# The middle tap of a three-tap convolution, moved from VectorE to ScalarE

## The chip, the cores and the metric

The kernel runs on one core of one Trainium2 chip. The metric is the device time of one execution in microseconds (us). Three runs of the kernel before took 1846.09 to 1850.96 us, median 1847.55. A core has five engines that matter here: TensorE (PE: matmuls and transposes), VectorE (DVE), ScalarE (ACT), GpSimd (POOL) and SyncE (SP, which issues DMAs). They run in parallel, each through its own list of instructions in order, and meet at semaphores. Matmul results land in eight PSUM banks; the rest is in SBUF, on 128 partitions.

## What is computed

The input `x` is 8 images of 512 channels and 32x32 tokens, f32. Four residual blocks follow each other, each on a group-normalized `x`: L0 (a 1x1 convolution with 25 correlations added to its inputs), L1 (the block that the change is in), and two plain 1x1 convolutions L2 and L3. L1, cut to what matters:

```python
xz = silu(einsum('oc,bchw->bohw', in_proj_w, x) + in_proj_b)      # 512 -> 1536 channels
x_ssm, res, gate = split(xz, 3, axis=1)
xf = x_ssm.reshape(B, 512, 1024)
xf = conv_general_dilated(xf, dw_w, (1,), [(1, 1)], feature_group_count=512) + dw_b   # 3 taps per channel
xf = silu(xf)
dbc = einsum('oc,bcn->bon', dbc_w, xf) + dbc_b                    # dt, B, C of a selective scan
y = selective_scan(gather(xf), softplus(dt), A, B, C, D)          # over a permutation of the tokens
y = scatter_back(y) * silu(gate) + res
out = silu(einsum('oc,bchw->bohw', out_proj_w, y) + out_proj_b)
```

The convolution of channel c at token n is w0 * x[n-1] + w1 * x[n] + w2 * x[n+1] + b, with zeros outside the 1024 tokens. The middle tap is w1 * x[n] + b.

## The kernel before

Channels lie on partitions, in 4 chunks of 128 (`KC`); tokens lie along the free dimension, 1024 of them, worked on in two halves of 512. The program of each engine is written out by hand, one `image` function per engine, run for images 0 to 7; the middle six run as a loop of two. `wait(eng, name, m, n)` holds an engine until semaphore `name` stands at the n-th event of image m. Nothing schedules: what stands first in an engine's text runs first.

The stage around the change is the head of an image. TensorE multiplies the 1536 output channels of the in projection in 24 units of 128 channels by 512 tokens; a unit is 12 f16 matmuls (`filler(1)`, in `in_step`, line 1467). Units 0 to 7 are `x_ssm`, two for each channel chunk. Between them stand `tokens(0)` to `tokens(3)`: for chunk k, 16 recorded small matmuls with `w_dbc` into bank 0 and 8 transposes (line 1620). Each waits for `conv_act`, the silu of its chunk.

ScalarE evicts each unit from PSUM (`in_evac`, line 599: silu with bias and a scale, into `conv_in`, which lies in `buf_b`, for units 0 to 7; into `gate` and `res` later). Between evictions come `conv_silu(m, k)` (line 607, in place on `conv_out[:, k % 2]`, which lies in `res`) and `tok_evac` (line 612, which copies the transposed tokens to `rows`). After unit 8 come an Exp and a Ln with their table loads (lines 641 and 643), half of the softplus of dt.

VectorE makes the three taps of chunk k, each a pass over 128x1024 f32: middle (line 1144, `tensor_scalar` with w1 and b), left (1146) and right (1148), the latter two as `scalar_tensor_tensor` that add onto `conv_out`. It begins a chunk when both halves are evicted (`in_evac` 2k + 2) and, from chunk 2, when TensorE has read the buffer two chunks back (`tok_mm`). After chunk 3 it does statistics of the next image, then softplus of dt, which raises `row_ready`; then GpSimd scatters the token rows in their permuted order to memory (line 450), SyncE reads them back, and VectorE (lines 1344 to 1362) and TensorE prepare the scan (line 1675).

In image 0 alone VectorE also ranks the tokens for the permutation (`ranks`, lines 1018 to 1038) ahead of the chunks: 1, 1, 1 and 2 steps. TensorE's later `gn_sum(m + 1, 0)` (a matmul of `st` and `cst`) waits for VectorE's statistics of the next image.

Of the kernel before, what the change touches and what calls it, by code (L numbers as in the profile page):

```python
# [8 lines left out]
ALU, ACT, AX = mybir.AluOpType, mybir.ActivationFunctionType, mybir.AxisListType  # L9
# [3 lines left out]
N = H * W  # L13
# [68 lines left out]
def build(nc, d):  # L82
    at, packed = constants()
    with ExitStack() as ctx:
        def sb(name, shape, dt=F32):
            return ctx.enter_context(nc.sbuf_tensor(name, shape, dt))

        def sem(name):
            return ctx.enter_context(nc.semaphore(name))
# [36 lines left out]
        par = sb("par", [P, 64])  # L126
# [16 lines left out]
        conv_in = buf_b[:, 0:KC * (N + 2)].rearrange("p (b n) -> p b n", b=KC)  # L143
        conv_out = res[:, 2:4, :]
# [51 lines left out]
        B0, BIN, BCONV, BOUT, BL2, BL3, TAP, WMAX, SCL, INV = 0, 4, 16, 20, 24, 28, 32, 44, 48, 52  # L196
# [12 lines left out]
        s = {n: sem(n) for n in names + gn_names}  # L209
# [19 lines left out]
        def wait(eng, name, m, n):  # L229

            if n:
                eng.wait_ge(s[name], m * per[name] + n)
# [278 lines left out]
        def _(eng):  # L511
            act = eng.activation
# [14 lines left out]
            scale = lambda name: par[:, SCL + WI[name]:SCL + WI[name] + 1]  # L527
# [62 lines left out]
            def in_evac(m, q):  # L590

                part, o, c = in_unit_at(q)
                wait(eng, "in_done", m, q + 1)
                if part == 0:
                    dst = conv_in[:, o, 1 + c.start:1 + c.stop]
                else:
                    dst = (gate, res)[part - 1][:, o, c]
                col = BIN + (0, 8, 4)[part] + o
                act(dst, ps[in_bank[q]][:, :], ACT.Silu, bias=par[:, col:col + 1], scale=inv("in")).then_inc(s["in_evac"], 1)  # L599
                if part == 1:  # L600

                    wait(eng, "in_evac", m, q + 1)
                    act(dst, dst, ACT.Silu).then_inc(s["silu2"], 1)

            def conv_silu(m, k):
                wait(eng, "conv_mac", m, 3 * k + 3)
                act(conv_out[:, k % 2, :], conv_out[:, k % 2, :], ACT.Silu).then_inc(s["conv_act"], 1)

            def tok_evac(m, k):
                wait(eng, "tok_mm", m, k + 1)  # L610
                for half in range(2):
                    ins = act(rows4[:, k // 2, 4 * half:4 * half + 4, (k % 2) * P:(k % 2) * P + P],
                              ps[tok_banks[k % 2][half]][:, :].rearrange("p (t c) -> p t c", t=4), ACT.Copy)
                ins.then_inc(s["tok_ev"], 1)

            def image(m, z, last=False):
# [5 lines left out]
                def filler(n):  # L622
                    for _ in range(n):
                        in_evac(m, next(fill))

                filler(3)
                conv_silu(m, 0)
                filler(2)
                conv_silu(m, 1)
                tok_evac(m, 0)  # L630
                filler(1)
                tok_evac(m, 1)
                filler(1)
                conv_silu(m, 2)
                filler(1)
                conv_silu(m, 3)
                tok_evac(m, 2)
                filler(1)
# [112 lines left out]
            for k in range(KC):  # L751
                normalize(0, 1, k, X[0])
            images(eng, image)

        @block.vector
        def _(eng):
            TT, TS, STT = eng.tensor_tensor, eng.tensor_scalar, eng.scalar_tensor_tensor
# [3 lines left out]
            m = mob[:, 0:8].rearrange("p (h c) -> p h c", h=HEADS)  # L761
# [215 lines left out]
            def rest_scales():  # L977

                eng.wait_ge(s["w_max"], 17)
                eng.tensor_reduce(par[:, 44:46], wmax[:, 9:17].rearrange("p (w k) -> p w k", k=KC), AX.X, ALU.max).then_inc(s["w_maxc"], 1)  # L980
                scales(2, 2, 2)
# [60 lines left out]
            def ranks(n):  # L1042

                for _ in range(n):
                    rank_step(*next(rank_order))
# [84 lines left out]
            def image(m, z, last=False):  # L1130
                first = is_first(m)

                for k in range(KC):
                    if first and k == 1:
                        rest_scales()
                    if first:
                        ranks((1, 1, 1, 2)[k])
                    wait(eng, "in_evac", m, 2 * k + 2)
                    wait(eng, "conv_pad", m, 1)
                    if k >= 2:  # L1140
                        wait(eng, "tok_mm", m, k - 1)
                    src, dst = conv_in[:, k, :], conv_out[:, k % 2, :]
                    w = [par[:, TAP + 3 * k + j:TAP + 3 * k + j + 1] for j in range(3)]
                    TS(dst, src[:, 1:N + 1], w[1], par[:, BCONV + k:BCONV + k + 1], ALU.mult, ALU.add).then_inc(s["conv_mac"], 1)
                    wait(eng, "conv_mac", m, 3 * k + 1)
                    STT(dst, src[:, 0:N], w[0], dst, ALU.mult, ALU.add).then_inc(s["conv_mac"], 1)  # L1146
                    wait(eng, "conv_mac", m, 3 * k + 2)
                    STT(dst, src[:, 2:N + 2], w[2], dst, ALU.mult, ALU.add).then_inc(s["conv_mac"], 1)  # L1148
# [308 lines left out]
            for k in range(KC):  # L1457
                split(0, 1, k)
                if k == 0:
                    ranks(1)  # L1460
            images(eng, image)


# [443 lines left out]
```

## Time and profile before

| what | value |
|---|---|
| median of three runs | 1847.55 us |
| lowest, highest | 1846.09, 1850.96 us |
| the profiled execution | 1856.14 us |
| its span (first to last instruction) | 1854.3 us |
| mean granted TensorE clock | 0.983 of full speed |
| TensorE busy | 1723.8 us, 93% |
| VectorE busy | 1097.6 us, 59% |
| ScalarE busy | 860.1 us, 46% |
| GpSimd busy | 416.3 us, 22% |

The rows further down come from one profiled execution; times in them are microseconds from the span's start, or nanoseconds where a mean is given. A timeline row is: start, duration, engine, line, operation, output <- inputs, count, and in brackets how long the engine sat idle before it and who ended that. An image takes about 217 us; image 0 has its convolution at 105 to 138 us, image 1 at 346, image 2 at 565, image 7 at 1647. Busy shares are averages: what an instruction is worth is read from the waits around it. Names in rows are those of the buffers, not of the views: `res<-buf_b,par` is a tap (`conv_out` from `conv_in`), `res<-res` is the convolution's silu, `buf_b<-bank,par` an eviction of units 0 to 7, `bank<-w_dbc,res` the first part of `tokens`.

### The profile page before, as it was taken

What the parts mean: (1) busy time and instruction counts of PE and PEld (TensorE: products, weight loads), DVE (VectorE), ACT (ScalarE), POOL (GpSimd) and SP (SyncE); (2) the same over time, 40 slices, a digit from 0 to 9 for tenths busy, and PEclk for the clock granted to TensorE, in tenths of its full rate; (3) what the DMA queues carried; (4) which work ended last, traced back from release to release, by engine and by line L of the source; (5) the groups of instructions that cost most, each with busy time, mean ns of one, the idle gap of its engine ahead of it and who ended that gap; (6) DMA issues with size and microseconds to landing.
All of it is one profiled execution on the core that took longest, in us unless ns stands there. A gap on an engine that the chain in (4) does not pass through costs nothing.

```text
span 1854.3 us, 23766 instructions
## 1 busy us (share of the span) xinstructions
PE 1723.8 (93%) x8573; PEld 951.1 (51%) x8573; DVE 1097.6 (59%) x2186; ACT 860.1 (46%) x1045; POOL 416.3 (22%) x425
## 2 busy tenths in 40 slices
PE   3576999999999999999999999999999999998988
PEld 2242654545545555456545565455554565454643
DVE  6777566544756547546665457565475456751665
ACT  3444544463445542555444644455425553444432
POOL 0403222043110330223210331103302231103220
PEclk9887999999999999999999999999999999999999
DMA  6202221133102331122311331023311233113201
GB/s 223 61 23 90 87 92 26 69 120 125 37 24 80 110 124 38 69 72 91 104 29 69 120 128 35 24 82 108 125 38 58 74 100 105 28 46 97 69 23 46
DMA packets 124634, 142.27 MB, mean 77 GB/s; under 512 B 52307, under 2 KB 101523, under 8 KB 124510
## 3 DMA queue, kind: packets, MB, share of 16 engines
q1 hardware_dynamic: 110462, 105.27, 17.9%
q0 software_dynamic: 12288, 34.68, 5.7%
q8 instruction: 72, 1.18, 0.3%
q10 hardware_dynamic: 1760, 0.71, 0.1%
q14 instruction: 52, 0.43, 0.1%
HBM read 80.62 MB, written 60.01 MB: 76 GB/s over the span
## 4 chain that ended last, share of the span: by engine, by line
PE 64%; DVE 12%; issue 7%; DMA 6%; ACT 4%; POOL 3%; another core or an unknown queue 3%; DVEq 0%; SPq 0%; POOLq 0%; ACTq 0%
PE bank L1467 61%; POOL d_scan L450 2%; DMA rows<-d_scan 2%; DMA rows<-d_norm 1%; DVE bn L850 1%; PE bank L1742 1%; PE bank L1675 1%; DMA d_scan<-rows,rank 1%; DVE gate L1212 1%; DVE gate L1023 1%; DVE res L1146 1%; PE bank L1620 1%; DVE res L1148 1%; DVE x_odd L1121 1%
## 5 line engine op out<-in xcount | busy, mean ns | idle before, releaser
L1467 PE MATMUL bank<-buf_a,win_hi 128*128 128x512 f16 x1536 | 463.2, 384 | 19.7 <-ACT gate L599 11.2
L1467 PE MATMUL bank<-buf_a,win_lo 128*128 128x512 f16 x768 | 294.0, 383 | 0.0
L1467 PE MATMUL bank<-buf_b,w_hi 128*128 128x512 f16 x960 | 287.9, 382 | 4.0 <-DVE buf_b L922 4.0
L1467 PEld LDWEIGHTS bank<-buf_a,win_hi 128*128 128x128 f16 x1536 | 149.7, 99 | 203.9 <-issue 28.4
L1467 PE MATMUL bank<-gate,w_out 128*128 128x512 f32 x512 | 228.9, 594 | 4.2 <-DVE gate L1214 4.2
L450 POOL DMA_INDIRECT d_scan<-rows,rank x128 | 125.2, 978 | 349.4 <-DVE rows L1183 313.5
L1467 PE MATMUL bank<-buf_b,w_lo 128*128 128x512 f16 x480 | 183.2, 382 | 0.0
L1467 PE MATMUL bank<-buf_a,w_hi 128*128 128x512 f16 x576 | 172.7, 381 | 1.8 <-DVE x_odd L1121 1.7
L467 POOL DMA_INDIRECT rows<-d_y,rank x128 | 123.0, 961 | 135.4 <-DMA d_y<-buf_b 89.7
L1467 PEld LDWEIGHTS bank<-buf_b,w_hi 128*128 128x128 f16 x960 | 94.1, 99 | 113.9 <-DVE buf_b L922 4.2
L1467 PEld LDWEIGHTS bank<-gate,w_out 128*128 128x128 f32 x512 | 94.5, 190 | 111.8 <-issue 99.5
L1212 DVE TENSOR_TENSOR gate<-bank,gate 128x512 f32<-128x512 f32 x64 | 44.0, 687 | 138.1 <-PE bank L1742 118.3
L1467 PEld LDWEIGHTS bank<-buf_a,win_lo 128*128 128x128 f16 x768 | 75.8, 99 | 93.1 <-issue 4.3
L599 ACT ACTIVATE res<-bank,par 128x512 f32<-128x512 f32 x64 | 48.9, 776 | 146.8 <-PE bank L1467 84.1
L394 POOL TENSOR_TENSOR st<-st,minus_half 128x4 f32<-128x4 f32 x30 | 31.0, 1032 | 364.0 <-DVE st L908 253.6
L1467 PE MATMUL bank<-buf_a,w_lo 128*128 128x512 f16 x288 | 109.7, 381 | 0.0
L922 DVE TENSOR_TENSOR buf_a<-work,buf_a 128x1024 f16<-128x1024 f32 x68 | 83.0, 1222 | 30.6 <-ACT work L553 30.3
L922 DVE TENSOR_TENSOR buf_b<-work,buf_b 128x1024 f16<-128x1024 f32 x60 | 73.4, 1223 | 41.6 <-ACT work L553 33.4
L1467 PE MATMUL bank<-buf_a 128*128 128x256 f16 (+1 forms) x768 | 83.8, 271 | 9.3 <-DVE buf_a L922 9.3
L599 ACT ACTIVATE buf_b<-bank,par 128x512 f32<-128x512 f32 x64 | 49.8, 778 | 91.8 <-PE bank L1467 91.7
L1467 PEld LDWEIGHTS bank<-buf_a,w_hi 128*128 128x128 f16 x576 | 56.4, 99 | 66.2 <-DVE x_odd L1121 2.2
L1467 PEld LDWEIGHTS bank<-buf_a 128*128 128x128 f16 x768 | 74.0, 100 | 20.8 <-issue 13.3
(225 smaller groups left out, 2822.3 us busy)
## 6 DMA issues: line engine op xcount, KB each, us to landing
rows<-d_scan SPq DMA_DIRECT2D x16, 1092.0 KB, 5.7
d_y<-buf_b SPq DMA_DIRECT2D x64, 256.0 KB, 2.1
work<-in_x SPq DMA_DIRECT2D x28, 512.0 KB, 4.4
d_gram<-rows SPq DMA_DIRECT2D x32, 260.0 KB, 2.6
x_even<-in_x SPq DMA_DIRECT2D x16, 512.0 KB
x_odd<-in_x SPq DMA_DIRECT2D x16, 512.0 KB
out_x<-x_even SPq DMA_DIRECT2D x16, 512.0 KB, 2.6
out_x<-x_odd SPq DMA_DIRECT2D x16, 512.0 KB, 2.6
```

The source lines that it names most:

```text
L394: eng.tensor_tensor(st[g][:, :, 4], st[g][:, :, 3], minus_half.broadcast_to([P, KC]), ALU.pow).then_inc(s[f"gn_rstd{g}"], 1)
L450: eng.indirect_dma_start(d_scan[h], bass.IndirectOffsetOnAxis(ap=rank[:, h, t:t + 1], axis=0), rows4[:, h, t, :], None).then_inc(s[f"scatt ...
L467: eng.indirect_dma_start(ytok[h][:, t, :], None, d_y[h], bass.IndirectOffsetOnAxis(ap=rank[:, h, t:t + 1], axis=0)).then_inc(s[f"y_in{h}{2 ...
L599: act(dst, ps[in_bank[q]][:, :], ACT.Silu, bias=par[:, col:col + 1], scale=inv("in")).then_inc(s["in_evac"], 1)
L850: eng.bn_stats(bn[g][:, k, half, :], x[:, k, half * HALF:(half + 1) * HALF]).then_inc(s[f"gn_raw{g}"], 1)
L922: TT(lo[:, k, :], normed[:, k % 2, :], hi[:, k, :], ALU.subtract).then_inc(s[f"gn_split{g}"], 1)
L1023: TS(cmp_row[:, :, start:start + n], others, own, 0.0, op, ALU.add, counts[:, a, q:q + 1]).then_inc(s["p_count"], 1)
L1121: STT(X[z][:, o, c], ps[(l2_bank if stage == 2 else l3_bank)[u]][:, :], par[:, INV + stage:INV + stage + 1], X[z][:, o, c], ALU.mult, ALU. ...
L1146: STT(dst, src[:, 0:N], w[0], dst, ALU.mult, ALU.add).then_inc(s["conv_mac"], 1)
L1148: STT(dst, src[:, 2:N + 2], w[2], dst, ALU.mult, ALU.add).then_inc(s["conv_mac"], 1)
L1212: TT(gate[:, k, c], ps[yt_bank[k][half]][:, :], gate[:, k, c], ALU.mult).then_inc(s["y_gate"], 1)
L1467: return eng.matmul(out, lhsT, rhs, start=start, stop=stop, skip_group_check=True, **kw)
```

## The change

The middle tap leaves VectorE and becomes a ScalarE activation (`Identity`, scale w1, bias b) in a new helper `mid_tap(k)`. It raises the same semaphore `conv_mac` as before, so the left tap on VectorE and everything behind it wait for the same counts. ScalarE's order gets four more instructions per image: middle taps 0, 1 and 2 stand directly behind the eviction that completes their chunk, middle tap 3 stands behind the eviction of unit 7 and in front of `conv_silu(m, 3)`. It waits for its own engine's eviction and, from chunk 2, for `tok_mm`.

```diff
-                filler(3)
+                def mid_tap(k):
+                    wait(eng, "in_evac", m, 2 * k + 2)
+                    if k >= 2:
+                        wait(eng, "tok_mm", m, k - 1)
+                    mid = par[:, TAP + 3 * k + 1:TAP + 3 * k + 2]
+                    act(conv_out[:, k % 2, :], conv_in[:, k, 1:N + 1], ACT.Identity, bias=par[:, BCONV + k:BCONV + k + 1],
+                        scale=mid).then_inc(s["conv_mac"], 1)
+
+                filler(2)
+                mid_tap(0)
+                filler(1)
                 conv_silu(m, 0)
-                filler(2)
+                filler(1)
+                mid_tap(1)
+                filler(1)
                 conv_silu(m, 1)
                 tok_evac(m, 0)
                 filler(1)
+                mid_tap(2)
                 tok_evac(m, 1)
                 filler(1)
                 conv_silu(m, 2)
                 filler(1)
+                mid_tap(3)
                 conv_silu(m, 3)
...
                     w = [par[:, TAP + 3 * k + j:TAP + 3 * k + j + 1] for j in range(3)]
-                    TS(dst, src[:, 1:N + 1], w[1], par[:, BCONV + k:BCONV + k + 1], ALU.mult, ALU.add).then_inc(s["conv_mac"], 1)
                     wait(eng, "conv_mac", m, 3 * k + 1)
```

ScalarE at the head of image 0, before, with the semaphores that each instruction waits for (`buf_b<-bank` is an eviction, `res<-res` the silu, `rows<-bank` an evacuation of tokens):

```order
L599 ACTIVATE buf_b<-bank,par 128x512 [waits in_done]
L607 ACTIVATE res<-res 128x1024 [waits conv_mac]
L599 ACTIVATE buf_b<-bank,par 128x512 [waits in_done]
L607 ACTIVATE res<-res 128x1024 [waits conv_mac]
L612 ACTIVATE rows<-bank 128x4x128 [waits tok_mm]
L612 ACTIVATE rows<-bank 128x4x128
L599 ACTIVATE gate<-bank,par 128x512 [waits in_done]
```

The same place, the last two chunks, with the change:

```order
L599 ACTIVATE buf_b<-bank,par 128x512 [waits in_done]
L607 ACTIVATE res<-res 128x1024 [waits conv_mac]
L599 ACTIVATE buf_b<-bank,par 128x512 [waits in_done]
L631 ACTIVATE res<-buf_b,par 128x1024 [waits tok_mm,in_evac]
L607 ACTIVATE res<-res 128x1024 [waits conv_mac]
L612 ACTIVATE rows<-bank 128x4x128 [waits tok_mm]
L612 ACTIVATE rows<-bank 128x4x128
L599 ACTIVATE gate<-bank,par 128x512 [waits in_done]
```

A middle tap now stands between the last eviction of `x_ssm` and the silu of chunk 3, and no table load stands beside it.

VectorE in image 0, before, from the end of the ranks of chunk 2 (`gate`, `sm`) over chunk 2's taps to the next rank step:

```order
L1030 TENSOR_REDUCE sm<-gate 128x1 [waits p_count]
L1144 TENSOR_SCALAR res<-buf_b,par 128x1024 [waits tok_mm,conv_pad,in_evac]
L1146 SCALAR_TENSOR_TENSOR res<-buf_b,par,res 128x1024 [waits conv_mac]
L1148 SCALAR_TENSOR_TENSOR res<-buf_b,par,res 128x1024 [waits conv_mac]
L1018 SCALAR_TENSOR_TENSOR gate<-res,md,cst 128x128 [waits p_count]
```

And with the change:

```order
L1041 SCALAR_TENSOR_TENSOR gate<-res,md,gate 128x128 [waits p_count]
L1044 TENSOR_REDUCE sm<-gate 128x1 [waits p_count]
L1159 SCALAR_TENSOR_TENSOR res<-buf_b,par,res 128x1024 [waits tok_mm,conv_mac,conv_pad,in_evac]
L1161 SCALAR_TENSOR_TENSOR res<-buf_b,par,res 128x1024 [waits conv_mac]
L1032 SCALAR_TENSOR_TENSOR gate<-res,md,cst 128x128 [waits p_count]
```

The chunk begins with the left tap, which has taken over the waits of the middle tap and waits for ScalarE through `conv_mac`.

## Rows read from the trace of the kernel before

**Rows 1.** The page's part 1, busy time (share of the span) and instructions, whole run.

```profile
PE 1723.8 (93%) x8573; PEld 951.1 (51%) x8573; DVE 1097.6 (59%) x2186; ACT 860.1 (46%) x1045; POOL 416.3 (22%) x425
```

**Rows 2.** Waits of the run: who waited for whom, total us, times, longest.

```profile
DVE res L1144 <- ACT buf_b L599: 93.8, 30, 4.3
...
PE bank L1467 <- DVE st L870: 48.3, 10, 17.7
```

**Rows 3.** Chain, window 540 to 790: start, us, what; the last convolution step.

```profile
588.39 0.79 ACT buf_b L599
589.20 0.82 DVE res L1144
590.05 1.30 DVE res L1146
591.37 1.29 DVE res L1148
...
601.45 1.06 POOL d_scan L450
```

**Rows 4.** TensorE in image 2: start, us, instruction [idle before <-releaser].

```profile
580.40 1.87 PE L1467 MATMUL bank<-w_dbc,res 128*128 128x34 f32 x16
...
593.80 1.98 PE L1467 MATMUL bank<-w_dbc,res 128*128 128x34 f32 x16 [0.25 <-ACT res L607]
...
602.23 0.60 PE L1467 MATMUL bank<-buf_a,win_hi 128*128 128x512 f16 x2 [0.37 <-ACT gate L599]
```

**Rows 5.** TensorE's `w_dbc` matmuls, images 1 to 7: idle before them, us, times.

```profile
  ACT res L607: 2.0, 7
```

**Rows 6.** Groups by line and form: x count, busy us, mean ns, idle.

```profile
L553 ACT ACTIVATE work<-x_odd,st 128x1024 f32<-128x1024 f32 x64 | 78.7, 1230 | 4.8 <-DVE buf_a L922 4.8
...
L607 ACT ACTIVATE res<-res 128x1024 f32<-128x1024 f32 x32 | 33.7, 1054 | 52.4 <-DVE res L1148 52.4
...
L1144 DVE TENSOR_SCALAR res<-buf_b,par 128x1024 f32<-128x1024 f32 x32 | 26.0, 813 | 93.8 <-ACT buf_b L599 93.8
```

**Rows 7.** ScalarE in image 2, timeline.

```profile
571.93 1.06 ACT L607 ACTIVATE res<-res 128x1024 f32<-128x1024 f32 x1 [0.94 <-DVE res L1148]
572.89 0.76 ACT L599 ACTIVATE buf_b<-bank,par 128x512 f32<-128x512 f32 x1
...
577.18 1.06 ACT L607 ACTIVATE res<-res 128x1024 f32<-128x1024 f32 x1 [1.00 <-DVE res L1148]
```

**Rows 8.** VectorE in image 0, timeline, middle taps 1 to 3.

```profile
118.68 0.80 DVE L1144 TENSOR_SCALAR res<-buf_b,par 128x1024 f32<-128x1024 f32 x1
...
124.90 0.81 DVE L1144 TENSOR_SCALAR res<-buf_b,par 128x1024 f32<-128x1024 f32 x1 [0.42 <-ACT buf_b L599]
...
133.86 0.81 DVE L1144 TENSOR_SCALAR res<-buf_b,par 128x1024 f32<-128x1024 f32 x1
```

**Rows 9.** TensorE in image 0, timeline, three waits.

```profile
123.27 1.97 PE L1467 MATMUL bank<-w_dbc,res 128*128 128x34 f32 x16 [0.90 <-ACT res L607]
...
138.46 1.97 PE L1467 MATMUL bank<-w_dbc,res 128*128 128x34 f32 x16 [1.93 <-ACT res L607]
...
173.71 0.59 PE L1467 MATMUL bank<-st,cst 128*128 128x8 f32 x2 [17.74 <-DVE st L870]
```

**Rows 10.** ScalarE in image 0, timeline, the eviction in front of middle tap 2.

```profile
124.08 0.78 ACT L599 ACTIVATE buf_b<-bank,par 128x512 f32<-128x512 f32 x1
```

**Rows 11.** TensorE, timeline, a wait in image 1 and in image 7.

```profile
447.80 0.70 PE L1467 MATMUL bank<-rows,work 128*128 128x256 f32 x2 [1.00 <-ACT buf_b L675]
...
1801.89 0.60 PE L1467 MATMUL bank<-buf_b,w_hi 128*128 128x512 f16 x2 [1.99 <-DVE buf_b L922]
...
1803.22 1.06 PE L1467 MATMUL bank<-buf_b,w_hi 128*128 128x512 f16 x2
```

**Rows 12.** TensorE, timeline, the wait at the scan's factors, images 4 and 5.

```profile
1060.54 1.09 PE L1675 MATMUL bank<-cst,x_odd 128*128 128x128 f32 x8 [0.31 <-DVE x_odd L1370]
...
1278.08 1.09 PE L1675 MATMUL bank<-cst,x_even 128*128 128x128 f32 x8 [2.03 <-DVE x_even L1370]
```

## The prediction

> **What bounds the kernel now.** I read the page's first part, then the list of who waited for whom, then the chain that ended last inside one image, then the timelines of TensorE, ScalarE and VectorE beside that piece of chain. TensorE is busy 93% of the span [rows 1], so a microsecond counts only where TensorE stands still for it, then or later. VectorE isn't the bound in general: before the instruction that this change removes, it sat idle 93.8 us over 30 of its 32 executions, waiting for ScalarE's eviction [rows 2]. The exception is image 0, where VectorE also ranks tokens: there TensorE once waits 17.7 us for VectorE's statistics [rows 2].
>
> Inside an image the convolution of channel chunk k is a serial path: eviction of the chunk's second half (ScalarE), middle tap, left tap, right tap (VectorE), silu (ScalarE), then `tokens(k)` on TensorE. For chunks 0 to 2 TensorE has other work queued in front of `tokens(k)`. For chunk 3 it hasn't enough: the chain of image 2 leaves TensorE at the last eviction (588.39), goes through the three taps (589.20, 590.05, 591.37), and goes on to softplus and GpSimd's first scatter at 601.45 [rows 3]. TensorE waits 0.25 us for that silu at 593.80, and 2.0 us in all over the seven images 1 to 7 [rows 4, 5]. So the path of chunk 3 is exactly on the edge: whatever is added to it, TensorE waits longer by that much.
>
> **The change, part by part.**
>
> *Removed:* 32 middle taps on VectorE at 813 ns, 26.0 us of its time [rows 6].
>
> *Added:* 32 ScalarE activations of the same 128x1024 f32 tile with a per-partition scale and a per-partition bias. The trace has just that form, the normalization into `work`: 1230 ns [rows 6]. The nearest other row is the silu of the same tile without either operand, 1054 ns [rows 6]. I take 1230 and keep 1054 as the lower bound; I know no row above 1230 for this size, so what could come on top is the handoff. ScalarE gets 32 x 1.23 = 39.4 us more. The order below shows no table load at the new line, so the function needs no other table than the silu around it.
>
> *Steady images, chunk 3.* Before, the middle tap starts at 589.20 and the next tap at 590.05: 0.85 us a step. A VectorE instruction begins 0.81 us after the start of the eviction that releases it (588.39 to 589.20), that is 0.03 after its 0.78 us. The new step has the same start (ScalarE's own next instruction, after its own eviction), lasts 1.23 and hands over in about 0.03: 1.26 us. The left and right taps and the silu slip by 1.26 - 0.85 = **0.41 us**. With 1054 ns it would be 0.24. What is queued behind on ScalarE is that silu itself, then an evacuation, the next eviction and the two table loads of softplus, all of which waited for the silu already: the whole row slips by the same 0.41. TensorE's later wait for ScalarE, 0.37 us at 602.23 [rows 4], doesn't grow, since both sides slip alike; nor does any wait of the scan, whose path starts from the scatter. The 0.41 is paid once an image: 7 x 0.41 = **+2.9 us**.
>
> *Steady images, chunks 0 to 2.* Silu 0 moves from 571.93 to 572.34. The eviction behind it followed by 0.96 us (572.89) and so moves to 573.30; it ends at 574.08. Middle tap 1 starts 0.03 later, at 574.11, and takes 1.26 to hand over, so VectorE starts at 575.37, runs two taps of 1.32 each (the step from 590.05 to 591.37) and lets silu 1 start at 578.01 instead of 577.18 [rows 7]; it ends at 579.07. TensorE asks for it at 580.40 [rows 4]: 1.3 us of cover are left. That is the tightest of the three; were it gone, each further tenth would be paid seven times. Chunk 2 stands alone between evictions, slips 0.41 on VectorE and ends in a silu that is behind an eviction anyway. Cost: nothing. The new waits hold nothing else up: in front of middle taps 2 and 3 ScalarE waits for `tok_mm` counts that TensorE has given microseconds before.
>
> *Image 0.* VectorE is late here, not idle: its middle taps 1 and 3 start the moment the ranks are done (118.68, 133.86), and TensorE waits 0.90 and 1.93 us for the silus behind them [rows 8, 9]. Middle tap 1 on ScalarE is long done by then; VectorE skips it and is 0.84 earlier. Then silu 1 and the eviction behind it (124.08 [rows 10]) come 0.84 earlier, at 123.24. Middle tap 2 starts 0.81 later, at 124.05, and releases VectorE at 125.31; before, that tap began at 124.90 + 0.85 = 125.75. The lead is now 0.44. In front of chunk 3 VectorE ranks again, without a pause, and skips tap 3: 0.44 + 0.85 = 1.29. From there VectorE works through to the statistics for which TensorE has waited 17.7 us at 173.71 [rows 9]; that row comes 1.29 earlier. TensorE reaches it earlier by as much, so the wait itself keeps its length, and all behind it gains. **-1.3 us**, once.
>
> *Sum:* +2.9 - 1.3 = **+1.6 us**. The profiled span of 1854.3 becomes 1855.9. The profiled execution (1856.14) lies some 9 us above the median of the three runs (1847.55), a difference that the change doesn't touch, so I set the sum on the median: 1849.1 us, 0.09% slower. About 0.3%, 5.5 us, is what a measurement of this kernel can tell from no change, so the verdict should be "the same".
>
> **A page against the rows.** The rows say that this operation is 0.41 us longer on ScalarE, and that VectorE was waiting before it in seven of eight images. The Trainium skill, Perfetto Trace Analysis, section Optimizing Scalar/DVE Operations, says that where the Vector engine has a faster mode for an operation it stays the faster place, and that handing it to the Scalar engine may pay where the Vector engine is saturated. By its first half each steady image loses, by its second image 0 gains; the trace agrees with both halves, 813 ns against 1230.
>
> **Rivals.**
>
> *1. The clock (slower).* TensorE's idle before the last `tokens` grows from 0.29 us on the average (2.0 over seven) to 0.70, followed by small matmuls. In image 7 the granted clock is lost after two idles of about 2 us: the one at 1801.89 is 1.99, and from 1803.22 two matmuls take 1.06 us instead of 0.60 [rows 4, 11], in three groups. Three matmuls then cost 0.46 x 1.5 = 0.69 more, a loss some 2.1 us in all, the level of 1.2 GHz in place of 2.4. If every steady image lost it after the longer idle: 7 x 2.1 = 14.7, and 1849.1 + 14.7 = 1863.8 us, 0.9% slower. It decides from the point where the idle is enough for a drop; against it stands the idle of 1.00 us at 447.80, after which the rows keep full speed [rows 11].
> [...]
>
> *2. The slip is absorbed (no change).* Further on, TensorE waits for the first scan factors, 2.03 us in image 5 and 0.31 in image 4 [rows 12]; of the six images with such a row (1 to 6) four are of the long kind. If what ends the long waits doesn't come from the convolution, the 0.41 disappears in those four images: 3 x 0.41 - 1.29 = -0.1, 1847.5 us. Against it: what VectorE works on there is rows that the scatter has written, and that starts 0.41 later.
>
> *3. These waits change their length.* The same wait differs by 1.7 us between images for no reason I can see in the program; it may hang on how GpSimd's scatters and TensorE's pieces fall together, and the slip may move an image from one kind to the other. Two images either way are 3.4 us: 1845.7 or 1852.5 us.
>
> *4. ScalarE's queue becomes the bound.* If ScalarE ran late by more than the 1.3 us at `tokens(1)`, TensorE would wait there too. It takes a middle tap of 2.5 us to get there; the price from that point is 7 us for each microsecond. At 1230 ns it isn't near.
>
> **How the numbers follow.** Forecast as summed, with either bound of the middle tap (0.24 x 7 - 1.3 = +0.4 to +2.9 if image 0 gave nothing): 0.70. Rival 1: 0.05. Rival 2: 0.09. Rival 3: 0.14. Rival 4: 0.02. The range takes in rival 3 on both sides and the spread of the runs themselves (1846.1 to 1851.0): **1844.5 to 1854.5 us**. Slower by over 0.3%: rivals 1 and 4, and the far end of 3, 0.08. Faster by over 0.3% needs image 0 and rival 3 at their best together: 0.03. Within 0.3%: 0.89.
>
> **What would show it.** In the changed profile: (a) a ScalarE row `res<-buf_b,par` 128x1024 x32 at about 1230 ns and no `TENSOR_SCALAR` of that shape on VectorE; (b) TensorE's wait before the last `tokens` of images 1 to 7 at about 0.7 each, some 4.9 us in all instead of 2.0; (c) from the last eviction of chunk 3 to its silu 4.7 us instead of 4.3; (d) in image 0 the first idle 0.90 nearly gone, the second near 1.5 instead of 1.93, and the statistics' matmul at 172.4 instead of 173.7; (e) the granted clock of 1.00 in the convolution stretch of each steady image. Wrong it would be if the middle tap took over 2.5 us, if the clock fell there, or if the scan waits moved.

## The result, and the profile after

The changed kernel took 1856.05 us in the median of 8 runs (1853.94 to 1860.63), the kernel before 1848.4 us in 8 runs beside them (1845.53 to 1852.41). The ratio is 1.0041 with an interval of 1.003 to 1.0051: 7.6 us slower, where 1.6 us (1849.1, at most 1854.5) had been forecast.

The spans of the two profiled executions don't show it: 1854.3 before, 1853.7 after. The profiled execution of before, 1856.14 us, lies well above its kernel's median; where that can come from is read in experiment a0. The comparison goes by the timed runs, and the traces are used for single stages.

The two groups that answer to [rows 6], by line and form (count, busy, mean ns, idle):

```profile
L1159 DVE SCALAR_TENSOR_TENSOR res<-buf_b,par,res 128x1024 f32<-128x1024 f32 x32 | 41.1, 1284 | 125.1 <-ACT res L631 123.3 <-PE bank L1633 1.8
...
L631 ACT ACTIVATE res<-buf_b,par 128x1024 f32<-128x1024 f32 x32 | 39.7, 1241 | 1.1
```

The middle tap takes 1241 ns, as forecast (1230), and VectorE now waits for it instead of for the eviction. TensorE's wait in front of the `w_dbc` matmuls, which answers to [rows 5] (idle, times):

```profile
  ACT res L607: 6.2, 7
```

It was 2.0 and is 6.2 us; 4.9 had been forecast. The piece of chain in image 2 that answers to [rows 3] (start, us, what):

```profile
586.23 0.79 ACT buf_b L599
587.04 1.25 ACT res L631
588.37 0.40 issue
588.76 1.30 DVE res L1159
590.08 1.29 DVE res L1161
...
600.15 1.06 POOL d_scan L450
```

From the eviction to the left tap it was 1.66 us (588.39 to 590.05), now it is 2.53 (586.23 to 588.76). Of the 0.87 more, 0.41 is the longer operation; the rest is the piece called issue: VectorE starts 0.47 us after the middle tap has ended (588.29), though the trace shows nothing else that holds it. Such a late start occurs in images 2, 4 and 6, where TensorE waits 1.12 us. In images 1, 3 and 5 VectorE follows within 0.04 us and TensorE waits 0.67; in image 7 it follows after 0.13 and TensorE waits 0.77.

What follows the wait is in the timeline of TensorE, image 2 (a `st,cst` matmul, the next image's group statistics, closes the stretch):

```profile
592.51 2.22 PE L1480 MATMUL bank<-w_dbc,res 128*128 128x34 f32 x16 [1.12 <-ACT res L607]
594.54 1.95 PE L1633 MATMUL bank<-cst,res 128*128 128x128 f32 x8
596.28 1.06 PE L1480 MATMUL bank<-buf_a,win_hi 128*128 128x512 f16 x2
...
609.84 0.28 PE L1480 MATMUL bank<-st,cst 128*128 128x8 f32 x2
```

and image 3:

```profile
810.87 1.97 PE L1480 MATMUL bank<-w_dbc,res 128*128 128x34 f32 x16 [0.67 <-ACT res L607]
812.67 1.07 PE L1633 MATMUL bank<-cst,res 128*128 128x128 f32 x8
...
827.08 0.28 PE L1480 MATMUL bank<-st,cst 128*128 128x8 f32 x2
```

In image 3 the 8 transposes take 1.07 us, in image 2 they take 1.95, and two f16 matmuls 1.06 (0.60 in [rows 4]). From the last tokens to the statistics' matmul it is 16.21 us in image 3 and 17.33 in image 2. In the kernel before it is 16.21 in each of images 1 to 6; image 2, after 593.80 in [rows 4]:

```profile
610.01 0.28 PE L1467 MATMUL bank<-st,cst 128*128 128x8 f32 x2
```

The granted clock of the two images, by windows of 10 us; the columns are window, its length, TensorE's busy time with its count, granted clock, DMA share, GB/s:

```profile
592.00:602.00 10.00, 9.49 (x48) 0.83 0.33 115
810.00:820.00 10.00, 8.95 (x53) 1.00 0.30 106
```

So in image 2 the clock fell from 2.4 to 1.2 GHz behind the longer wait, for a loss of 17.33 - 16.21 = 1.12 us. It also fell in image 7, behind 0.77. In images 4 and 6 the wait is the same 1.12 us as in image 2, and the stretch is 16.21: no fall. In image 0 (rows that answer to [rows 9]) the first wait is gone, and the statistics' matmul comes 1.69 us earlier; 0.54 of that TensorE was ahead already at the first tokens (114.69 instead of 115.23), which leaves 57.33 us instead of 58.48 from there:

```profile
136.79 1.97 PE L1480 MATMUL bank<-w_dbc,res 128*128 128x34 f32 x16 [1.66 <-ACT res L607]
...
172.02 0.59 PE L1480 MATMUL bank<-st,cst 128*128 128x8 f32 x2 [18.31 <-DVE st L884]
```

### The profile page after: what moved, and what is told of

Its sections match the earlier page's. It is cut to its first block, busy times and chain, and to the rows that moved or that the text cites. A ratio compares the mean times of both kernels' runs of the same rounds, so it can differ in the third digit from the quotient of the medians.

```text
span 1853.7 us, 23789 instructions
## 1 busy us (share of the span) xinstructions
PE 1725.3 (93%) x8573; PEld 952.5 (51%) x8573; DVE 1074.0 (58%) x2154; ACT 900.1 (49%) x1077; POOL 415.6 (22%) x425
## 4 chain that ended last, share of the span: by engine, by line
PE 69%; DVE 11%; issue 6%; ACT 5%; DMA 4%; POOL 2%; another core or an unknown queue 2%; DVEq 0%; SPq 0%; POOLq 0%; ACTq 0%
PE bank L1480 66%; POOL d_scan L450 1%; DMA rows<-d_norm 1%; DVE bn L864 1%; PE bank L1688 1%; PE bank L1755 1%; DMA rows<-d_scan 1%; DVE gate L1037 1%; PE bank L1633 1%; DVE gate L1225 1%; DVE res L1159 1%; DVE res L1161 1%; ACT res L631 1%; ACT rows L612 1%
## 5 line engine op out<-in xcount | busy, mean ns | idle before, releaser
L1159 DVE SCALAR_TENSOR_TENSOR res<-buf_b,par,res 128x1024 f32<-128x1024 f32 x32 | 41.1, 1284 | 125.1 <-ACT res L631 123.3
L572 ACT ACTIVATE corr<-bank 96x512 f16<-96x512 f32 x16 | 9.5, 592 | 161.3 <-PE bank L1537 161.3
```

## The experiments

The clock column is the mean granted clock over all runs of that kernel, the waits are those of images 1 to 7 in front of the last tokens, summed in the profiled execution, and the falls are the stretches of images 1 to 6 from the last tokens to the statistics' matmul that took 17.3 instead of 16.2 us (b3, c3 and c4 put other work into this stretch, 16.0, 15.6 and 18.0 us in all six images; none has a fall). Each group of four ran on a chip of its own, with the kernel before beside it (mean clock 0.9824, 0.9835, 0.9812). Ratios of different groups compare poorly: a2 and c2 differ by one middle tap, that of chunk 3 in image 0, and their ratios by 0.0034.

| kernel | median us | before us | ratio (interval) | clock | waits | falls |
|---|---|---|---|---|---|---|
| after | 1856.05 | 1848.4 | 1.0041 (1.0030 to 1.0051) | 0.9791 | 6.2 | 1 |
| a0 | 1851.07 | 1848.45 | 1.0013 (1.0004 to 1.0022) | 0.9820 | 2.0 | 0 |
| a1 | 1856.43 | 1848.45 | 1.0043 (1.0030 to 1.0056) | 0.9802 | 5.1 | 3 |
| a2 | 1850.65 | 1848.45 | 1.0008 (0.9998 to 1.0018) | 0.9830 | 2.0 | 0 |
| a3 | 1844.01 | 1848.45 | 0.9978 (0.9967 to 0.9989) | 0.9822 | 2.0 | 0 |
| b1 | 1860.05 | 1846.79 | 1.0069 (1.0051 to 1.0087) | 0.9778 | 5.0 | 3 |
| b2 | 1853.97 | 1846.79 | 1.0042 (1.0025 to 1.0059) | 0.9828 | 1.4 | 0 |
| b3 | 1845.64 | 1846.79 | 1.0002 (0.9987 to 1.0017) | 0.9825 | 0 | 0 |
| b4 | 1859.31 | 1846.79 | 1.0066 (1.0053 to 1.0080) | 0.9792 | 4.7 | 4 |
| c1 | 1864.01 | 1862.11 | 1.0013 (0.9998 to 1.0028) | 0.9807 | 3.7 | 1 |
| c2 | 1857.89 | 1862.11 | 0.9974 (0.9960 to 0.9988) | 0.9813 | 2.0 | 0 |
| c3 | 1854.39 | 1862.11 | 0.9958 (0.9943 to 0.9972) | 0.9815 | 0 | 0 |
| c4 | 1849.87 | 1862.11 | 0.9937 (0.9916 to 0.9958) | 0.9833 | 0 | 0 |

### a0: the kernel before, again

> The kernel before, unchanged, profiled and timed again. Theory S (the slip at chunk 3 is stretched by a longer handoff from ScalarE to VectorE and by the granted clock, which falls after the longer wait in some images): ratio 1.000 within its interval, and in its trace no fall of the granted clock behind the last tokens of images 1 to 7, a mean granted clock near 0.983. Rival P (the first trace of before is not typical, and its plain executions lose less time at the scan's waits): the span of this trace is near 1846, not 1854, and the difference lies in waits other than the one at the last tokens.

The ratio of the kernel to itself came out as 1.0013, with an interval that leaves out 1. So a difference of 0.1 or 0.2% is not told from nothing here, whatever its interval says, and the other verdicts are read with that. Its trace has no fall of the clock behind the last tokens of images 1 to 7. Its span is 1849.3, not 1846, and its waits in front of the scan's first transposes (two an image, line 1675, images 1 to 7; us, times) are

```profile
  DVE x_odd L1370: 6.6, 5
  DVE x_even L1370: 6.0, 4
```

where the first trace of the same kernel had

```profile
  DVE x_even L1370: 12.5, 6
  DVE x_odd L1370: 6.1, 6
```

18.6 against 12.6 us: these waits vary by several microseconds between executions of one kernel, which is more than the 5.0 by which the spans differ. Theory S stands, and rival P is half right: the first trace was not typical, by such waits.

The traces show one place where the two part. VectorE's copy of the next image's statistics (line 901) needs only TensorE's `st,cst` matmul, but in the first trace it starts 2.62 to 2.67 us after that matmul in images 1 to 6, and 1.51 to 1.58 us after the end of GpSimd's eighth scatter; in a0 it starts 0.04 to 1.14 us after the matmul. GpSimd's other eight scatters stand behind it and begin 3.40 to 3.48 us after the end of the first eight in the first trace, 1.26 to 1.95 in a0. Why the copy starts late was not tested.

### a1, a2, a3: parts of the change

```diff
+        def on_act(first, k):
+            return k == 3          # a1;  a2: k < 3;  a3: first
...
+                    if not on_act(first, k):
+                        TS(dst, src[:, 1:N + 1], w[1], par[:, BCONV + k:BCONV + k + 1], ALU.mult, ALU.add).then_inc(s["conv_mac"], 1)
```

The helper `mid_tap` returns at once where `on_act` is false.

> Only the middle tap of chunk 3 goes to ScalarE, in all images; chunks 0 to 2 keep theirs on VectorE. Theory S: this carries nearly the whole loss, ratio 1.003 to 1.005; the waits before the last tokens are 0.67 and 1.1 us. In image 0 it still gains 0.85 us. Rival Q (the loss is ScalarE's load at chunks 0 to 2, or more work on ScalarE anywhere): ratio below 1.002.

> The middle taps of chunks 0 to 2 go to ScalarE, that of chunk 3 stays on VectorE. Theory S: no loss, about 0.4 us gained in image 0, ratio 0.999 to 1.001, and the waits before the last tokens stay at 0.25 to 0.34 us. Rival Q: ratio above 1.002.

> All four middle taps on ScalarE in image 0 alone, on VectorE in images 1 to 7. By the sum of the prediction a gain of 1.3 us, ratio 0.9993; the statistics' matmul of image 0 comes 1.3 to 1.7 us earlier. If the gain of image 0 is lost later, ratio 1.000.

Chunk 3 alone carries the whole loss (1.0043); chunks 0 to 2 cost nothing that can be told from the kernel against itself. Rival Q falls: ScalarE's load isn't the point. The waits in a1 are 0.67 to 0.78, not 1.1: VectorE follows the middle tap within 0.14 us in images 1 to 7. In a1 the clock fell in three of six images; image 4, TensorE:

```profile
1024.82 2.13 PE L1488 MATMUL bank<-w_dbc,res 128*128 128x34 f32 x16 [0.77 <-ACT res L611]
...
1028.49 1.06 PE L1488 MATMUL bank<-buf_a,win_hi 128*128 128x512 f16 x2
```

All four taps in image 0 alone made it faster by 4.4 us, more than the 1.3 of the sum. From the first tokens of image 0 to its statistics' matmul it takes 57.36 us instead of 58.48 (58.46 in a0), so the trace has 1.12 us of it; where the rest is, or whether it is the scatter seen in a0 (b3 has the same image 0, 57.36 us, and shows no gain), stays open.

The gains that were expected in image 0 of a1 (0.85 us) and a2 (0.4) are not in their traces: the same stretch takes 60.46 and 59.28 us. Nor is it fixed for one program: b2 has the image 0 of after and takes 59.78 us where after takes 57.33. In b2 TensorE waits 1.72 us at the second tokens and the granted clock is 0.50 from 123 to 129 us; in after it is 0.56 from 117 to 120, ahead of these tokens, and 1.00 from 120 on. With one program the two are 2.45 us apart, and what the rows show of the difference is when the clock fell.

### b1 and c1: only a delay

```diff
+                if not first:
+                    wait(eng, "conv_mac", m, 12)
+                    act(idle_room[:, :], conv_out[:, 1, 0:232], ACT.Copy).then_inc(s["slip"], 1)
+                    wait(eng, "slip", m, 1)
                 conv_silu(m, 3)
```

All middle taps are on VectorE; `idle_room` is read by nobody. In c1 the copy has 8 columns. Image 0 gets a copy of 8 columns in front of its first silu.

> The kernel before, with one small ScalarE copy of 128x232 put between VectorE's last tap and the silu of chunk 3 in images 1 to 7, and the silu made to wait for it: a slip of about 0.4 us at the same place, with all middle taps on VectorE. Theory S (what costs is the longer wait in front of the last tokens, in itself and through the granted clock that falls behind it in some images): the waits are 0.65 to 0.75 us, falls of the clock appear behind them, mean clock 0.980, ratio 1.003 to 1.005. Rival R (only the slip costs, the clock is as it was): ratio 1.0015, mean clock 0.983. Rival M (it is something about the middle tap on ScalarE): ratio 1.000 to 1.0015.

> As b1_before_plus_delay, but the copy is 128x8: the silu of chunk 3 slips by about 0.2 us, the waits in front of the last tokens are 0.45 to 0.6 us. If falls of the clock need a wait of more than that (none was seen behind waits up to 0.48 us, some behind 0.67 to 1.12), the stretch from the last tokens to the statistics' matmul is 16.21 us in each of images 1 to 6, the mean clock 0.983, and the ratio 1.000 to 1.0015, 7 x 0.2 us. If already this wait is enough, some stretches are 17.34 us and the ratio is 1.002 or more.

b1 is the whole loss again, and more, without a middle tap on ScalarE. TensorE in image 2:

```profile
594.60 1.97 PE L1475 MATMUL bank<-w_dbc,res 128*128 128x34 f32 x16 [0.68 <-ACT res L608]
...
597.32 1.06 PE L1475 MATMUL bank<-buf_a,win_hi 128*128 128x512 f16 x2
...
611.95 0.28 PE L1475 MATMUL bank<-st,cst 128*128 128x8 f32 x2
```

A wait of 0.68 us, then 1.06 for two matmuls, and a stretch of 17.35 us. Rivals R (0.983 expected, 0.9778 measured) and M are out. Image 0 has a small copy too, and its stretch takes 60.11 us instead of 58.48. Why b1 lost some 13 us isn't all accounted for: 3.0 of longer waits, four falls in its trace (image 7 included) of 1.13 and 1.6 in image 0 make 9.1. By the mean clock, as an estimate, span times the difference to the kernel before, 0.0057 x 1858, is 10.6 us, more than the falls behind the last tokens.

c1, with waits of 0.49 and 0.58 us, had one fall, in image 5, behind a wait of 0.58. My bound of "over 0.48" held, but the ratio of 1.0013 can't be told from a0's.

### b2 and b3: TensorE works while it would wait

```diff
                 filler(1)
+                if not first:
+                    piece(1)
                 tokens(3)
-                filler(5)
+                if first:
+                    filler(5)
+                else:
+                    piece(5 * KC - 1)
```

> The changed kernel, but in images 1 to 7 TensorE does 3 matmuls (0.65 us) of the next unit in front of the last tokens instead of behind them. Theory S: the wait falls from 0.67 and 1.12 to about 0.02 and 0.5, the falls of the clock there become rare, mean clock 0.982, ratio to the kernel before near 1.001. Rival R (the later convolution path delays the scan, and filling TensorE doesn't help): ratio stays at 1.003 to 1.005, with longer waits at the scan.

> Middle taps on ScalarE in image 0 alone, and the same 3 matmuls moved in front of the last tokens in images 1 to 7. A candidate for a faster kernel: if the waits of 0.25 and 0.34 us are all that is to be had, 2 us less than image 0 alone, ratio 0.997; if the last tokens come 0.3 us later and the scan then waits, no more than image 0 alone, 0.998.

b2 took away 4.8 of 6.2 us of waits:

```profile
  ACT res L607: 1.4, 3
```

and all falls of the clock (0.9828), and yet the time stayed at 1.0042. The work that TensorE did early came back as waiting at the scan's transposes, images 1 to 7:

```profile
  DVE x_even L1383: 12.3, 7
  DVE x_odd L1383: 9.1, 6
```

21.4 us, against 15.8 in the changed kernel:

```profile
  DVE x_odd L1383: 10.0, 6
  DVE x_even L1383: 5.8, 5
```

So rival R of this run is right, and theory S was only half of it: there are two edges at this place. Beside b3, on the same chip, which differs by the middle taps of images 1 to 7 alone, b2 is 8.3 us slower in the median at the same mean clock (0.9828 and 0.9825). Their traces differ by 10.4 us of span, and 9.8 of it is in three places: 6.0 at the scan's transposes (15.4 us in b3), 1.4 at the tokens and 2.4 in image 0. So the later path of chunk 3 costs its microseconds without a fall behind the last tokens, too. The last tokens also start the row path (softplus, scatter, reading back), whose end the scan waits for. Filling TensorE doesn't help while the row path is late. b3 says the same: no waits at the tokens, no gain.

### b4: fewer waits in front of the left tap

```diff
-                    wait(eng, "in_evac", m, 2 * k + 2)
-                    wait(eng, "conv_pad", m, 1)
-                    if k >= 2:
-                        wait(eng, "tok_mm", m, k - 1)
                     src, dst = conv_in[:, k, :], conv_out[:, k % 2, :]
```

> The changed kernel without VectorE's waits for the eviction, the pads and the token matmuls in front of the left tap; ScalarE's middle tap, for which it still waits, comes behind all of them. If the 0.45 us by which the left tap of chunk 3 starts late in images 2, 4 and 6 comes from working through these waits, it goes (left tap 0.03 behind the middle tap), the waits in front of the last tokens are 0.67 us in all of images 1 to 7, and the time falls by 1.3 us or more if the clock gains too. If not, nothing changes.

The waits are 0.67 or 0.68 in all seven images:

```profile
  ACT res L607: 4.7, 7
```

So the late start in images 2, 4 and 6 is gone with these waits. They are not enough to make it: in a1 the left tap of chunk 3 has the same four and starts at most 0.14 us after the middle tap. The time didn't fall: four of six images lost the clock, and the ratio is 1.0066.

### c2: all but chunk 3 of images 1 to 7

The function `on_act` returns `first or k < 3`.

> The changed kernel, but with the middle tap of chunk 3 back on VectorE in images 1 to 7: ScalarE makes 25 of the 32 middle taps. Theory S: nothing is left of the loss, the gain of image 0 stays: no falls of the clock, waits 0.25 to 0.34 us, ratio 0.998 to 1.000. Rival Q (ScalarE's load costs): ratio 1.002 or more.

0.9974: with 25 of 32 middle taps on ScalarE nothing is lost. Its trace has no fall behind the last tokens and the waits of the kernel before. Whether it is a gain is less sure than the interval says: a2, one tap less, came out at 1.0008 on another chip. The loss hangs on seven taps.

### c3 and c4: a shorter path at chunk 3

The taps and the silu of chunk 3 are made in two parts, columns 0 to 509 behind unit 6 and 510 to 1023 behind unit 7. All taps are on VectorE.

```diff
+                    if k == KC - 1:
+                        for part, (c0, c1) in enumerate(((0, CUT), (CUT, N))):
+                            if part:
+                                wait(eng, "in_evac", m, 2 * k + 2)
+                            n = 3 * k + 3 * part
+                            TS(dst[:, c0:c1], src[:, c0 + 1:c1 + 1], w[1], par[:, BCONV + k:BCONV + k + 1], ALU.mult, ALU.add).then_inc(s["conv_mac"], 1)
...
-                conv_silu(m, 3)
+                for part, (c0, c1) in enumerate(((0, CUT), (CUT, N))):
+                    wait(eng, "conv_mac", m, 12 + 3 * part)
+                    act(conv_out[:, 1, c0:c1], conv_out[:, 1, c0:c1], ACT.Silu).then_inc(s["conv_act"], 1)
```

c4 has this too, ScalarE's `filler(1)` moved behind `tok_evac(m, 3)`, and on TensorE:

```diff
-                filler(1)
+                piece(2)
                 tokens(3)
-                filler(5)
+                piece(6 * KC - 2)
```

> The kernel before, with chunk 3 cut in two at token 510: its first part is convolved and put through the silu as soon as unit 6 is evicted, so that behind unit 7 only 514 of 1024 tokens are left. The path from the last eviction to the end of the silu becomes about 1.9 us shorter. Theory S turned round: the waits in front of the last tokens vanish (2.0 us in all), the row path starts 0.3 us earlier, ratio 0.998 to 0.999. If the wait isn't on the path: 1.000.

> As c3_split_chunk3, and the last tokens stand 6 matmuls (1.3 us) earlier on TensorE, with the eviction of unit 8 behind the softplus on ScalarE. If the waits at the scan's factors (1 to 2 us in most images) hang on the convolution's path through the scatter, they shrink by up to 1.6 us in six images: ratio 0.994 to 0.997. A wait of TensorE for the eviction of unit 8, up to 1 us an image, may take that back: then 0.998 to 1.002.

c3 is faster by 0.42%, more than its 2.0 us of waits; the surplus isn't explained. Its trace, of an execution 5.3 us above its median, waits 28.2 us at the scan's transposes, the most of all: as in b2, what TensorE saves at the tokens comes back there. c4 is the fastest kernel of the study, 0.63% below the kernel before. Its ScalarE in image 2:

```profile
586.43 0.78 ACT L600 ACTIVATE buf_b<-bank,par 128x512 f32<-128x512 f32 x1 [0.87 <-PE bank L1481]
587.10 0.62 ACT L639 ACTIVATE res<-res 128x510 f32<-128x510 f32 x1
589.40 0.63 ACT L639 ACTIVATE res<-res 128x514 f32<-128x514 f32 x1 [1.68 <-DVE res L1156]
```

From the last eviction to the end of the silu it is 3.6 us (586.43 to 590.03), where it was 5.36 (588.39 to 593.75, by [rows 3] and the 1.06 of [rows 7]). TensorE takes the last tokens 0.1 us later, without a wait, and pays 0.88 for the eviction of unit 8, as expected:

```profile
590.13 1.93 PE L1481 MATMUL bank<-w_dbc,res 128*128 128x34 f32 x16
...
597.73 0.60 PE L1481 MATMUL bank<-buf_a,win_hi 128*128 128x512 f16 x2 [0.88 <-ACT gate L600]
```

What it gets for that is at the scan's transposes:

```profile
  DVE x_odd L1384: 2.7, 4
  DVE x_even L1384: 1.0, 3
```

3.7 us, where c2 and c3 on the same chip have 20.6 and 28.2. Two things made room, in image 2: from the last tokens to the first scatter it is 6.82 us instead of 7.65 (590.13 to 596.95; 593.80 to 601.45 in [rows 4] and [rows 3]), and TensorE has 17.97 us of work and waiting to the statistics' matmul instead of 16.21. So these waits are what is left of the row path from the last tokens once TensorE has run out of work; c4 changes both sides at once, and which counts for more isn't separated.

## Why the prediction was wrong

**What bounds the kernel** was read rightly as far as it went: the path of chunk 3 is on the edge (a1 against a2), images 1 to 7 lose and image 0 gains in after, chunks 0 to 2 have cover. That the scan is a second edge behind it (b2) was not seen.

**The steady images, chunk 3.** The operation was right (1241 against 1230 ns). "Hands over in about 0.03" failed in four of seven images: it was 0.48 or 0.49 us in three and 0.13 in image 7. The sum for the waits was +2.9 and is 6.2 - 2.0 = +4.2.

**Image 0.** 1.15 us (1.69 less the 0.54 ahead) against 1.3. The closeness is in part luck: b2, with the same image 0, takes 2.45 us longer there.

These two give +3.0 instead of +1.6; the forecast would have stayed inside its range.

**The step that failed is the clock, which the sum put at nothing.** As rival 1 it got a chance of 0.05, on the strength of one row, the wait of 1.00 us at 447.80 that kept full speed. The clock did fall, not in every image as the rival was priced but in some: behind waits of 0.67 to 1.12 us, in 11 of 24 stretches (after, a1, b1, b4), and behind waits up to 0.48 us in none of 42 (six images each of before, a0, a2, a3, b2, b3, c2). One fall costs 1.13 us in the rows, not 2.1. At 11 in 24, seven images lose 7 x 0.46 x 1.13 = 3.6 us, and 3.0 + 3.6 = 6.6 of the 7.6; with the two falls of the trace of after it is 2.3, and 5.3 of the 7.6. The mean clock of the runs, 0.9791 against 0.9812 to 0.9835 for the kernel before, is by the same estimate 4 to 8 us of span. A single row that escaped a rare event was taken as a bound; the question was how often, and the price should have been a mean. The sum of 4.2, of the 1.15 and of the falls is what the runs show in its place.

How sure that is: a1, a2, b1 and c2 show that the slip at chunk 3 makes the loss. The clock's share is an estimate and no run isolates it. One measure of all falls is TensorE's busy time times (1 - granted clock), summed over stretches of 2 us from 200 us to the end. It is 5.3 and 6.4 us in the two traces of the kernel before, 8.9 in after, 12.3 in a1, 12.9 in b1, 9.8 in b4 and 1.5 in b2. But b2, with the least, still has the ratio 1.0042, because the late row path took the place of the falls. Taking the clock's falls away is not shown to give their time back.

**Rival 2** (absorbed) is out: b1 and a1 pay for the slip. **Rival 3** is true of single executions (18.6 and 12.6 us in two traces of one kernel), but these waits aren't without reason, as I had written: b2 and c4 show that they hang on the row path, and a0 shows one place in it that differs between executions. **Rival 4** didn't occur.

**Setting the sum on the median** was sound in arithmetic and hid a warning: a profiled execution 8 us above the median of its kernel isn't a fair picture of its waits.

## What to carry to other kernels

An operation may move to an idle engine only where its path has slack; ask that of each instance, not of the loop: here 25 of 32 could go without loss and 7 could not. A wait of TensorE that grows from 0.3 to 0.7 us costs its own length and, in a share of the cases, the clock behind it, so price it as a chance times the loss, from several traces if they can be had. Filling one wait helps only if the path behind it isn't the next to be waited for (b2). Where a path is on the edge, look for a way to shorten its last step (c3) and give TensorE work to do behind it (c4, 0.63%); that c3 beats c2 can't be told, their intervals overlap.

## What the runs showed of the hardware that I had not expected

The clock fell behind a wait of 0.58 us (c1) and stayed up behind waits of 0.67 to 1.12 in 13 of 24 cases. A `scalar_tensor_tensor` on VectorE with four waits started 0.48 or 0.49 us after the last of them was met in images 2, 4 and 6 of after and of b2, 0.13 or 0.14 in image 7 and at most 0.04 in 1, 3 and 5; in a1, with the same four, it was 0.13 or 0.14 in images 2, 4, 6 and 7 and at most 0.04 in the others; with one wait it was at most 0.04 in all seven (b4). VectorE's small copy of statistics started 2.62 to 2.67 us after the matmul it needed in before, which is 1.51 to 1.58 us after the end of GpSimd's eighth scatter, and within 1.14 us in a0. And a kernel timed against itself differed by 0.13% outside its interval (a0).
